# Graph network: the weighing of the last layer with its operands exchanged

## The reference, cut to what matters

```
for h in range(8):
    Wx = x @ Ws[h] + Wb[h]
    s = Wx[v_tgt] @ a_w[h, :d] + Wx[v_src] @ a_w[h, d:] + a_b[h]
    s = leaky_relu(s, 0.2)
    alpha = segment_softmax(s, v_tgt, n)
    outs.append(segment_sum(alpha[:, None] * Wx[v_src], v_tgt))
out = layernorm(x + stack(outs).reshape(n, -1))
```

## Time and profile before

| | us |
|---|---|
| median of the runs (lowest, highest) | 2272.47 (2269.34, 2274.48) |
| profiled execution, its own time | 2274.44 |
| its span | 2272.7 |
| the 80 steps of the last layer, first score to last weighing | 1992.1 to 2254.9 |

### The profile page before, as it was taken

The page is one execution under the profiler, slowest core; times in us unless marked ns, Lnnn a source line. Parts: engine busy times, 40 slices in busy tenths (PEclk is TensorE's granted clock), DMA queues, the critical chain, the costliest instruction groups (busy, mean ns, idle before and its releaser), DMA issues. The chain is left out here.

```text
span 2272.7 us, 39837 instructions
## 1 busy us (share of the span) xinstructions
PE 2066.5 (91%) x15006; PEld 1608.6 (71%) x15006; DVE 1573.7 (69%) x3095; ACT 957.0 (42%) x1444; POOL 665.8 (29%) x488
## 2 busy tenths in 40 slices
PE   5999979899899999899999899999898996978886
PEld 4899937788788888788888787888785554433332
DVE  6789754778764778764777765678855235699985
ACT  0222213666333666433666433666420023045444
POOL 0000015300554200554210554200350000088785
PEclk9999989999999999999999999999999997999998
DMA  2000041789711698811688812588963300000001
GB/s 75 24 25 36 32 143 60 133 143 154 157 47 52 120 151 144 171 44 55 112 150 149 177 34 65 99 147 148 205 153 90 68 12 22 0 1 1 0 1 46
DMA packets 490381, 195.82 MB, mean 86 GB/s; under 512 B 441767, under 2 KB 460199, under 8 KB 490195
## 3 DMA queue, kind: packets, MB, share of 16 engines
q1 hardware_dynamic: 490195, 193.31, 41.8%
HBM read 62.94 MB, written 25.45 MB: 39 GB/s over the span
## 5 line engine op out<-in xcount | busy, mean ns | idle before, releaser
L720 PE MATMUL psum<-turned_probability_parts,values_high 125*128 125x125 bf16 x1600 | 278.6, 221 | 49.9 <-DMA turned_probability_parts<-probability_parts 23.2
L922 DVE CUSTOM_DVE_ANT_0 probabilities<-psum,counts 125x1250 f32<-125x1250 f32 x160 | 233.5, 1460 | 114.9 <-PE psum L722 114.6
L1480 ACT ACTIVATE probabilities<-probabilities,row_peaks 125x1250 f32<-125x1250 f32 x160 | 214.5, 1341 | 176.2 <-DVE row_peaks L926 176.2
L722 PE MATMUL psum<-turned_probability_parts,values_low 125*128 125x125 bf16 x1600 | 277.8, 220 | 0.0
L721 PE MATMUL psum<-turned_probability_parts,values_high 125*128 125x125 bf16 x1600 | 277.6, 220 | 0.0
L1680 DVE SCALAR_TENSOR_TENSOR probability_parts<-probabilities,row_masses,probability_parts 125x1250 bf16<-125x1250 f32 x160 | 251.6, 1573 | 13.5 <-ACT probability_parts L1492 13.3
L2033 POOL TENSOR_TENSOR logs_and_shifts<-logs_by_source,target_shifts_spread 125x1250 f32<-125x1250 f32 x80 | 208.2, 2619 | 107.3 <-ACT target_shifts_spread L2190 67.9
L1492 ACT ACTIVATE probability_parts<-probabilities,row_masses 125x1250 bf16<-125x1250 f32 x160 | 214.1, 1338 | 46.4 <-DVE row_masses L934 43.1
L2307 PE MATMUL psum<-probabilities_turned,values_and_ones 125*65 125x512 f32 (+1 forms) x480 | 190.1, 540 | 23.5 <-ACT probabilities_turned L2208 13.1
L720 PEld LDWEIGHTS psum<-turned_probability_parts,values_high 125*128 125x128 bf16 x1600 | 158.0, 99 | 73.8 <-issue 67.9
L2307 PEld LDWEIGHTS psum<-probabilities_turned,values_and_ones 125*65 125x65 f32 x480 | 63.6, 142 | 136.2 <-issue 113.7
(11 more groups left out here) (335 smaller groups left out, 5061.0 us busy)
## 6 DMA issues: line engine op xcount, KB each, us to landing
weight_stage<-in_L_gnn_m_w SPq DMA_DIRECT2D x32, 256.0 KB, 2.9
block_inputs_kept<-nodes SPq DMA_DIRECT2D x8, 896.0 KB
counts_kept<-counts_by_target_rows SPq DMA_DIRECT2D x10, 625.0 KB, 3.1
logs_kept<-counts SPq DMA_DIRECT2D x1, 5468.8 KB
nodes<-block_inputs_kept SPq DMA_DIRECT2D x12, 448.0 KB
turned_probability_parts<-probability_parts SPq DMA_TRANSPOSE x320, 3.6
counts_by_target<-counts_kept SPq DMA_DIRECT2D x2, 2187.5 KB
logs_by_source<-logs_kept SPq DMA_DIRECT2D x1, 4375.0 KB
```

Source lines behind the costliest of these rows:

```text
L720: pe.matmul(out, lh, rh, start=first, stop=False, skip_group_check=True)
L722: return pe.matmul(out, ll, rh, start=False, stop=last, skip_group_check=True)
L922: dve.tensor_tensor_reduce(prob[0:TILE, T % 2, :], scores, fx.count_src[0:TILE, i, 0:NODES], scale, MASKED, ALU.add, ALU.max, p[:, 0:1]).t ...
L1480: nc.scalar.activation(prob[0:TILE, T % 2, :], prob[0:TILE, T % 2, :], ACT.Exp, bias=fx.peak[0:TILE, T % 2, 1:2], accum_out=fx.mass[0:TILE ...
```

## The change

The operands of the weighing change places: the probabilities of 125 sources x 125 targets are loaded, and the 65 columns of `values` stream. A step is now ten matmuls (twenty instructions) in place of three (six), and the sums come out with the targets on the partitions: 125 x 65 for each of ten row tiles, five in a bank. The halves (h, k) take turns in banks 0, 1 and 2 (`rows_bank`). So the copy of the sums, the transposes, the `weighted` tile and their semaphores go. The mass and its reciprocal stay on VectorE, now at j = 1 and 2. The scaling moves to ScalarE (`scaled_part`), five passes of 125 x 64 each half, behind the exponential of j = 1 and 2. `parted` counts row tiles. The weighing waits, before it writes a bank anew, until the half three before has been scaled. `shift_turned` no longer waits for `parted`.

```diff
+        def rows_bank(h, k):
+            return bank((2 * h + k) % 3)
...
             def join(h, k):
-                pool.wait_ge(parted, 2 * h + k + 1)
+                pool.wait_ge(parted, HALF * (2 * h + k + 1))
...
             def out_part(h, k):
-                view = back_bank(h, k)[0:TILE, 0:HALF * WIDTH].rearrange("p (t d) -> p t d", d=WIDTH)
+                view = rows_bank(h, k)[0:TILE, 0:HALF * WIDTH].rearrange("p (t d) -> p t d", d=WIDTH)
-                dve.wait_ge(back, n + 1)
+                if n >= 2:
+                    dve.wait_ge(parted, HALF * (n - 1))
+                dve.wait_ge(pv, TILES * (h + 1))
                 dve.tensor_scalar(m, view[:, :, HDIM3:WIDTH]..., 1e-30, None, ALU.max).then_inc(part_own, 1)
                 dve.wait_ge(part_own, 2 * n + 1)
                 dve.reciprocal(v, m).then_inc(part_own, 1)
-                dve.wait_ge(part_own, 2 * n + 2)
-                if h >= 1:
-                    dve.wait_ge(joined, n - 1)
-                dve.tensor_tensor(part[0:TILE, k], view[:, :, 0:HDIM3], v.unsqueeze(2).broadcast_to([TILE, HALF, HDIM3]),
-                                  ALU.mult).then_inc(parted, 1)
...
-                if h >= 1 and j in (3, 4):
-                    out_part(h - 1, j - 3)
+                if h >= 1 and j in (1, 2):
+                    out_part(h - 1, j - 1)
...
-            dve.wait_ge(pv, STEPS)
-            a, z = CUTS[1]
-            dve.tensor_copy(weighted[0:WIDTH, (HEADS3 - 1) % 2, a:z], region(0)[0:WIDTH, a:z]).then_inc(last_copied, 1)
...
-            def copy_out(h):
-                act.wait_ge(pv, TILES * (h + 1))
-                if h >= 2:
-                    act.wait_ge(back, 2 * h - 2)
-                for a, z in ((0, NODES),) if h < HEADS3 - 1 else CUTS[0::2]:
-                    nc.scalar.activation(weighted[...], region(0)[...], ACT.Copy).then_inc(out_copied, 1)
+            def scaled_part(h, k):
+                n = 2 * h + k
+                act.wait_ge(part_own, 2 * n + 2)
+                if h >= 1:
+                    act.wait_ge(joined, n - 1)
+                for t in range(HALF):
+                    at = t * WIDTH
+                    nc.scalar.activation(part[0:TILE, k, t, :], rows_bank(h, k)[0:TILE, at:at + HDIM3], ACT.Copy,
+                                         scale=inverse[0:TILE, k, t:t + 1]).then_inc(parted, 1)
...
-                if j == 0 and h >= 1:
-                    copy_out(h - 1)
+                if h >= 1 and j in (1, 2):
+                    scaled_part(h - 1, j - 1)
...
             def shift_turned(h):
...
-                elif h == 1:
-                    pe.wait_ge(piece_copied, 4)
                 else:
-                    pe.wait_ge(parted, 2 * h - 2)
+                    pe.wait_ge(piece_copied, 4 * h)
...
             def weigh(T):
                 h, j = T // TILES, T % TILES
                 pe.wait_ge(exped, T + 1)
-                if j == 0 and h >= 1:
-                    pe.wait_ge(out_copied, h)
-                for a, z in CUTS:
-                    mm = pe.matmul(region(0)[0:WIDTH, a:z], values[0:TILE, j, h, :], prob[0:TILE, T % 4, a:z],
-                                   start=(j == 0), stop=(j == TILES - 1))
+                for t in range(TILES):
+                    k, at = t // HALF, (t % HALF) * WIDTH
+                    if j == 0 and t % HALF == 0 and 2 * h + k >= 3:
+                        pe.wait_ge(parted, HALF * (2 * h + k - 2))
+                    mm = pe.matmul(rows_bank(h, k)[0:TILE, at:at + WIDTH], prob[0:TILE, T % 4, cols(t)], values[0:TILE, j, h, :],
+                                   start=(j == 0 and t % HALF == 0), stop=(j == TILES - 1), skip_group_check=True)
                 mm.then_inc(pv, 1)
...
-                if h >= 1 and j in (2, 3):
-                    turn_back(h - 1, j - 2)
             weigh(STEPS - 1)
-            for k in range(2):
-                turn_back(HEADS3 - 1, k)
```

More of the change, by code:

```diff
@@ L1959, in fourth_layer @@
         offset = packer(nc, SLOT_A_AT + TILES * NODES * 4 + 16)("logs_and_shifts", [128, 2, NODES], F32)
-        weighted = packer(nc, LAST_AT)("weighted_values_turned", [128, 2, NODES], F32)
         stored = sem("stored")
@@ L1972, in fourth_layer @@
         offset_ready, scored, exped, pv = sem("offsets_ready"), sem("scored"), sem("exped"), sem("weighted")
-        out_copied, last_copied, back = sem("weighted_copied"), sem("last_weighted_copied"), sem("weighted_turned_back")
         part_own, parted, joined = sem("part_or_row_scale_step"), sem("parts_ready"), sem("nodes_joined")
@@ L1990, in region @@
             return psum[:, n * BANK:n * BANK + NODES]
-        def back_bank(h, k):
-            return bank(6 if (h, k) == (HEADS3 - 1, 1) else 7)
+        def rows_bank(h, k):
+            return bank((2 * h + k) % 3)
         def reach_of(h):
@@ L2190, in shift_piece @@
                 nc.scalar.activation(shifts[0:TILE, h % 2, a:z], bank(7)[0:TILE, 0:z - a], ACT.Copy).then_inc(piece_copied, 1)
-            def copy_out(h):
-                act.wait_ge(pv, TILES * (h + 1))
-                if h >= 2:
-                    act.wait_ge(back, 2 * h - 2)
-                for a, z in ((0, NODES),) if h < HEADS3 - 1 else CUTS[0::2]:
-                    nc.scalar.activation(weighted[0:WIDTH, h % 2, a:z], region(0)[0:WIDTH, a:z], ACT.Copy).then_inc(out_copied, 1)
+            def scaled_part(h, k):
[7 more added lines that the diff above has]
+                                         scale=inverse[0:TILE, k, t:t + 1]).then_inc(parted, 1)
             shift_turned(0)
@@ L2216, in _ @@
                         shift_piece(h + 1, j - 5)
-            copy_out(HEADS3 - 1)
+            for k in range(2):
+                scaled_part(HEADS3 - 1, k)
             for k in range(2):
@@ L2284, in shift_piece @@
                 mm.then_inc(piece, 1)
[L2286 to L2299, removed]
             def weigh(T):
```

## The result

The changed kernel takes 2411.73 us (median of 4 runs, 2411.34 to 2412.63); the kernel before, run beside it, 2272.71 us (4 runs, 2269.34 to 2274.48). The ratio is 1.0614, with a 95% interval of 1.0596 to 1.0633: 139 us slower, where 9.7 us faster was forecast. The time lies outside the range, too, and on the side of rival A (2391 us).

A forecast was written before the change was run, and what follows sets the result against it. VectorE was taken to set the pace in the last layer's 80 steps; -7.7 (VectorE), -1.0 (j = 7), -1.0 (seventh head) and 0 (tail) gave -9.7 us, 2262.8 us on the median. Range 2254 to 2380 us.

The forecast's parts named there:

- rival A: Last layer's 80 steps: loading doesn't keep the clock up, TensorE stays at 1.2 GHz and becomes the bound; +119, 2391 us; chance 0.36.
- twenty instructions at 0.11 us: New weighing on TensorE: 2.2 us a step, at most 2.4, with the load setting the pace.
- TensorE's part: Weighing 0.1 us more a step, 1.0 a head, against ten transposes less, 1.1 to 1.3 us; unseen where TensorE has room.
- VectorE's part: Scaling (0.82 us) and the wait for transposes (0.71) leave VectorE: 1.53 us less a head, 7.7 us over five heads.
- The bank stop: First weighing of a head waits for ScalarE to scale half 0; 1.9 us of room before step 4, costs nothing.
- rival B: TensorE, idle some 2.6 us at the bank, comes late as the clock falls again each head; total -1.7, 2271 us; chance 0.11.
- The shift transpose and j = 7: Transpose 0.87 us earlier, no longer waiting for the part; VectorE's wait at j = 7: -1 us, between -3.4 and +1.2.
- Case C: Idle time at the shift transpose gets too short for a clock fall; -13.3, 2259 us, down to 2254; chance 0.11.
- The seventh head: TensorE ends the chain here; earlier step 4 and transpose, less longer weighings: -1.0 us (0 to -2).
- Small passes and the tail: ScalarE passes 0.35 us, back to back 0.26 to 0.35; behind the last weighing 0 us, between -0.2 and +0.7.
- The scaling on ScalarE: Moving the output parts' scaling from VectorE to ScalarE, twice a head: 0.82 us less a head.

The follow-up runs named there:

- e1: The changed kernel with each weighing matmul streaming 100 columns of values in place of 65, same loads; 2269.63 us, ratio 0.9981 to the kernel before.
- e9: The kernel before with eight float32 matmuls in the gap at the shift transpose, each loading 125 columns and streaming 2; 2274.26 us, ratio 1.0007.
- e10: The kernel before with eight float32 matmuls in the gap at the shift transpose, each loading 125 columns and streaming 125; 2269.3 us, ratio 0.9978.
- e7: e1 with ScalarE's scaling passes ahead of the exponential of j = 1 and 2, VectorE's order kept; 2255.96 us, ratio 0.9925 to the kernel before.
- e4: e1 with the scaling of the output parts back on VectorE, one pass a half; 2298.02 us, ratio 1.009 to the kernel before.
- e8: The kernel before with only the scaling moved to ScalarE, five passes a half at j = 3 and 4; 2276.06 us, ratio 1.0013.
- e5: The changed kernel with two more matmuls in each weighing, each loading 64 columns and streaming 187; 2576.14 us, ratio 1.1335 to the kernel before.
- e6: e1 with ScalarE's passes ahead of the exponential and VectorE's mass and reciprocal ahead of the score; 2272.41 us, ratio 0.9983 to the kernel before.
- e11: The changed kernel with e5's added matmuls, sixteen wide matmuls ahead of the first weighing, and ScalarE's passes ahead of the exponential; 2570.08 us.
- e2: The changed kernel with sixteen float32 matmuls of 512 columns ahead of the first weighing, so the loop starts at the full clock; 2419.37 us.
- e3: The changed kernel with each weighing matmul streaming 80 columns in place of 65; 2411.81 us, ratio 1.0604 to the kernel before.

## Why the prediction was wrong, step by step

**What failed is the term "twenty instructions at 0.11 us" in TensorE's part.** The rows it came from the earlier trace rows were short runs of such instructions at 2.4 GHz. The number itself is right at that clock (5.70 / 50 in e1), but it was put into a sum as if the clock were given. In the changed kernel the granted clock was 0.50 from the first weighing to the last, and there an instruction takes 0.21 us, as in the earlier trace rows. A weighing took 4.3 us for the 2.2 of the forecast, 2.1 us more a step where 0.1 was counted, and TensorE became the bound with 51.1 us a head. e1 has the same loads and instructions with 100 columns streamed, and there the clock came up and the 142 us were gone.

**Rival A was the right mechanism, with less chance than the forecast.** Its argument against itself was "TensorE would have some instruction at work 2.2 us of each step's 3.2, more than in the stretch before the fall". e9 shows that this counted the wrong thing: 3.80 of 3.80 us at work, and the clock fell. So the busy time of the earlier trace rows and that of the new weighing, whose loads fill 95% of the time, could not be compared. The Trainium skill (TensorE: Matmul & The Clock Gate, "What's actually happening") ties the clock to how busy TensorE has been recently. The traces agree for falls behind a wait (1.78 us in the earlier trace rows); in e9 the clock fell behind a stretch that the profile lists as busy for all of 3.80 us, so what that view calls busy is not enough.

**Rival A's price was 20.7 us too low**, nearly all of it by three terms: a head's weighings take 42.8 us (42 said), the shift pieces 5.1 (4.2), the spreads and transposes 3.2 (2): 51.1 for 48 us, and over eight heads 402.4 for 382. The range ended at 2380, below the 2391 of the rival itself, to which I gave 0.36: at that chance its price belonged inside.

**VectorE's part (-1.53 us a head) was right, where the clock is up.** e10 takes the falls out of the kernel before and gives its head without them: 33.05 us, as long as the one such head, the second, in the kernel before itself. Less 1.53 that is 31.52; e7 has 31.50. That it fits to 0.02 us is luck: against e10, steps j = 1 and 2 of e7 are 0.26 and 0.21 us longer and not 0.42 each for mass and reciprocal, and step 4 is still 0.1 to 0.4 us above the 4.84 that it takes in e4 (4.8 said). j = 3 took 2.05 to 2.32 us (2.2 said). In the changed kernel the gain is there and worth nothing: VectorE waits 19.5 us of each head of 51.09, and what is left is 31.6.

**The bank stop was not free.** The prediction gave it 1.9 us of room, by the end of the first weighing at 7.9 us against step 4 at 9.8. It overlooked that the weighings of j = 1 and 2 had piled up behind the stop and that L2258 is queued behind these too: fifty instructions and 5.7 us. In e1 step 4 is 5.6 us without a fall and 7.0 or 7.2 with one; in e7, with the stop a microsecond shorter, 5.0 to 5.2. It is rival B's place, and its idle time of 2.05 us (2.6 said) is what the clock falls behind in e1. That the shorter stop is what keeps the clock up in e7 is argued from this pair: both came with one edit.

**The shift transpose and j = 7.** The forecast of -1 lay between a loss of 1.2 and a gain of 3.4. Where the clock stays up, step 7 is 3.87 us for 4.82 and the whole 0.86 is gone (e1, e7, and e10 with nothing else changed). Case C's reasoning was right for the kernel at the full clock, where its price, 2259 us and down to 2254, takes in e7's 2255.96; as e7 is another kernel than the changed one, this is no hit. The seventh head, for which -1.0 us (0 to -2) was forecast, is 2.7 us shorter in e7 (29.73 for 32.44). And a term was missing that no case had: the loop begins at the low clock, where the new weighing takes 4.2 us, so that the first head is 1.1 us longer in e7 and 1.9 in e1 than the 32.18 before.

**Small passes and the tail.** A pass takes 0.31 us on average, and back to back they begin 0.20 apart (ten in 2.15 in the tail): 0.35, and 0.26 to 0.35, were too dear. So the joins are done at 3.5 us behind the masses and the root isn't late: -0.8 us where 0 was forecast, outside the bounds of -0.2 and +0.7.

**The scaling on ScalarE** was forecast to give 0.82 us a head as part of the whole. By itself it gives nothing (e8), since the shift transpose waits for it; with the new places and the three banks it gives 0.6 (31.86 in two heads of e1 for 32.46 in one of e4).

What stays open is why 80 columns leave TensorE at 1.2 GHz from start to end and 100 don't, and why e5, with as many streamed columns as e1, stays there too. The runs show the two outcomes and none between them in one kernel's medians, but e1, e4 and e6 move between the two levels within a run. Whether the changed kernel, with 65 columns, could hold the full clock if TensorE never paused was not tried.

## What to carry to other kernels

Before a matmul is turned round so that it streams fewer columns for each load, price it at both clock levels. Don't take TensorE's busy share for a sign of the clock (e9, e11); if the slow price makes TensorE the bound, take it for the likely one until a run shows otherwise. A few unused columns streamed behind each load may cost nothing (0.11 us an instruction with 100 columns at the full clock) and here were worth 142 us. Streaming about as much in two extra matmuls a weighing was worth nothing (e5). And where a semaphore stops an in-order queue, count everything that piles up behind the stop before the instruction for which another engine waits, and look where the queue will stand idle next: e4 and e6 freed the bank and got the wait at the shift transpose instead.

## What the runs showed of the hardware

- Eight matmuls of loads with next to no stream didn't hold the clock: in two stretches alike in the profile (PE 3.80 of 3.80 us, PEld 3.00 and 3.05) it fell behind 2 streamed columns a load (e9) and stayed up behind 125 (e10).
- The clock can fall without a gap: in e11 at 2021.3 us, the last wait of TensorE having ended at 2008.5.
- At the lower level an instruction with 125 columns loaded takes about twice as long: 0.11 us at 2.4 GHz (e1, 5.70 us for fifty), 0.21 at 1.2 (changed kernel, 42.8 us for two hundred).
- The low state can be one from which a kernel never gets out: the changed kernel and e2 have TensorE busy without a gap for 380 us and more at 1.2 GHz, e3 for 390, e5 and e11 for 450 and 528. More work put beside the loads (e5) only made it dearer: 71.24 us a head for 51.09.
- ScalarE passes of 125 x 64 from PSUM, with the scale from a column, overlap: 0.31 us each in the mean, and back to back one begins every 0.20 us.
